# A third value tap moves from VectorE to GpSimd, and the null parts follow the subtraction for x

## What is computed

```
x = x + proj(attention(q, k, v))            # on the group-normalised x
kv = dw3x3(einsum(qkv_w, x)); k, v = split(kv)   # 3x3 depthwise convolution, nine taps per channel
q  = idwt2(dw3x3(dwt2(x)))                  # wavelets, three sets of 3x3 taps
attn = softmax(normalised q @ normalised k.T * temperature)   # 8 heads of 16 channels
```

## Time and profile before

| | us |
|---|---|
| median of 3 runs | 1373.13 |
| lowest and highest run | 1371.81, 1376.18 |
| the profiled execution, its whole time | 1372.45 |
| its span in the trace | 1370.8 |
| TensorE busy | 1157.9 |
| VectorE busy | 1008.8 |
| ScalarE busy | 803.8 |
| GpSimd busy | 533.8 |

### The profile page before, as it was taken

The page is one execution under the profiler, slowest core; times in us unless marked ns, Lnnn a source line. Parts: engine busy times, 40 slices in busy tenths (PEclk is TensorE's granted clock), DMA queues, the critical chain, the costliest instruction groups (busy, mean ns, idle before and its releaser), DMA issues. The chain is left out here.

```text
span 1370.8 us, 36304 instructions
## 1 busy us (share of the span) xinstructions
PE 1157.9 (84%) x12648; PEld 920.4 (67%) x12648; DVE 1008.8 (74%) x1801; ACT 803.8 (59%) x1414; POOL 533.8 (39%) x369
## 2 busy tenths in 40 slices
PE   0899937999999899998999999846999997999900
PEld 0555527889999899998999999724555554555500
DVE  6777517999999899998999999525777774163494
ACT  0677735777777676775777677202444445766382
POOL 6200004577687676876668686602000001000010
PEclk9999977999999999998999999866999999999955
DMA  9976783545544535445355354155777633000079
GB/s 325 416 298 262 296 196 88 138 108 123 148 106 120 136 93 147 132 99 137 98 135 144 102 132 112 40 211 185 248 262 262 231 92 121 1 0 0 1 300 406
DMA packets 148805, 221.21 MB, mean 161 GB/s; under 512 B 115746, under 2 KB 116892, under 8 KB 144296
## 3 DMA queue, kind: packets, MB, share of 16 engines
q1 hardware_dynamic: 137560, 152.23, 37.0%
q0 software_dynamic: 6480, 47.19, 9.1%
q10 hardware_dynamic: 4608, 19.67, 4.1%
HBM read 131.82 MB, written 87.20 MB: 160 GB/s over the span
## 5 line engine op out<-in xcount | busy, mean ns | idle before, releaser
L1693 PE MATMUL b_conv_bank<-b_sign,wsign 128*128 (+1 forms) x1728 | 299.7, 327 | 7.7 <-ACT b_sign L1491 7.5
L982 DVE SCALAR_TENSOR_TENSOR b_value_sum<-b_vin,b_vtaps,b_value_sum 128x576 f32<-128x576 f32 x320 | 259.3, 810 | 14.4 <-ACT b_value_sum L908 13.6
L1693 PEld LDWEIGHTS b_conv_bank<-b_sign,wsign 128*128 128x128 bf16 x1728 | 168.0, 97 | 144.6 <-issue 31.4
L936 ACT CAST b_feat<-b_bank 96x400 f16<-96x400 f32 x255 | 125.5, 492 | 184.9 <-PE b_bank L1026 184.9
L1024 PE MATMUL b_bank<-b_tkh,b_kt 96*96 96x100 f16 x1536 | 224.3, 211 | 2.5 <-DVE b_tml L1005 2.2
L1025 PE MATMUL b_bank<-b_tkl,b_kt 96*96 96x100 f16 x1536 | 223.7, 211 | 0.0
L1026 PE MATMUL b_bank<-b_tkh,b_kt 96*96 96x100 f16 x1536 | 223.7, 211 | 0.0
L1024 PE MATMUL b_bank<-b_yh,b_tmh 96*96 96x200 f16 x768 | 195.2, 254 | 30.8 <-DVE b_feat L989 11.0
L1024 PEld LDWEIGHTS b_bank<-b_tkh,b_kt 96*96 96x96 f16 x1536 | 195.2, 127 | 4.2 <-DVE b_tml L1005 2.5
L1026 PEld LDWEIGHTS b_bank<-b_tkh,b_kt 96*96 96x96 f16 x1536 | 195.3, 127 | 0.0
L1025 PEld LDWEIGHTS b_bank<-b_tkl,b_kt 96*96 96x96 f16 x1536 | 193.8, 126 | 0.0
(11 more groups left out here) (232 smaller groups left out, 2522.7 us busy)
## 6 DMA issues: line engine op xcount, KB each, us to landing
b_vin<-value_projection_scratch SPq DMA_DIRECT2D x32, 686.0 KB, 5.1
keys_scratch<-b_khl SPq DMA_DIRECT2D x24, 784.0 KB, 3.5
value_projection_scratch<-b_vout ACTq DMA_DIRECT2D x24, 784.0 KB, 4.7
b_kt<-keys_scratch SPq DMA_DIRECT2D x128, 147.0 KB, 3.3
b_xraw<-in_x SPq DMA_DIRECT2D x128, 144.0 KB, 4.8
values_scratch<-b_vacc SPq DMA_DIRECT2D x32, 576.0 KB, 3.2
values<-values_scratch SPq DMA_DIRECT2D x48, 384.0 KB, 3.7
out<-xs SPq DMA_DIRECT2D x25, 576.0 KB, 6.8
```

What stands on the lines that cost most here:

```text
L936: nc.scalar.copy(*target(n, 0, k)).then_inc(s_hi, 1)
L982: nc.vector.scalar_tensor_tensor(whole if t == DVE_TAPS[-1] else part, src, vtaps[:, t:t + 1], part, ALU.mult, ALU.add).then_inc(s_tap, 1)
L1693: ins = nc.tensor.matmul(cbank[k % NBK][:, 0:CH].rearrange("p (r c) -> p r c", c=W), p["wsign"][nth // NIMG][:, t * C:(t + 1) * C], padded ...
```

## The change

VectorE keeps taps 1 to 5 (10 instructions a group instead of 12) at an even spacing; GpSimd takes taps 6, 7 and 8 (three products and three additions a slab instead of two and two). In `body`, `low_x(i+1)` now stands ahead of `edges`.

```diff
-        DVE_TAPS = (1, 2, 3, 4, 5, 6)
-        POOL_TAPS = (7, 8)
+        DVE_TAPS = (1, 2, 3, 4, 5)
+        POOL_TAPS = (6, 7, 8)
         NTAP = 2 * len(DVE_TAPS)
         PSTEPS = 2 * len(POOL_TAPS)
-        TAP_AT = (0, 2, 3, 5, 7, 8, 10, 12, 13, 15, 17, 18)
+        TAP_AT = (0, 2, 4, 6, 8, 10, 12, 14, 16, 18)
...
                 pool.wait_ge(s_ptap, i * PSTEPS + 1)
                 pool.sem_inc(s_carry, 1)
                 add_product(slot)
-                pool.wait_ge(s_ptap, i * PSTEPS + 2)
-                pool.sem_inc(s_carry, 1)
-                product(slot, POOL_TAPS[1])
-                pool.wait_ge(s_ptap, i * PSTEPS + 3)
-                pool.sem_inc(s_carry, 1)
-                add_product(slot)
-                pool.wait_ge(s_ptap, i * PSTEPS + 4)
+                for n, t in enumerate(POOL_TAPS[1:]):
+                    pool.wait_ge(s_ptap, i * PSTEPS + (2 * n + 2))
+                    pool.sem_inc(s_carry, 1)
+                    product(slot, t)
+                    pool.wait_ge(s_ptap, i * PSTEPS + (2 * n + 3))
+                    pool.sem_inc(s_carry, 1)
+                    add_product(slot)
+                pool.wait_ge(s_ptap, i * PSTEPS + PSTEPS)
                 pool.sem_inc(s_carry, 1)
...
                     spread_taps(i + 2, k % 2)
+                if how != LAST:
+                    low_x(i + 1, (k + 1) % 2)
                 if head is not None:
                     edges(head, k // GPH % 2 ^ 1, i)
-                if how != LAST:
-                    low_x(i + 1, (k + 1) % 2)
                 first_product(i, k % 2)
```

## The result

The changed kernel takes **1412.8 us** (median of 4 runs, 1411.66 to 1421.59), against 1374.2 us for the kernel before on the same chip: a ratio of 1.0296, 95% interval 1.0251 to 1.0341. It is slower, as predicted, but by 38.6 us where the prediction had 15, and outside its range of 1379 to 1402 us.

The account below looks back on a forecast made before the run. GpSimd was taken to become the bound at 84.48 us a head: 1372.45 us profiled plus 10.2 gave 1382.7, plus 6 for the two jumps 1388.7, rounded to 1388 us; range 1379 to 1402 us.

Parts of the forecast that it names:

- GpSimd sets the pace: GpSimd's chain: the added pair costs 5.11 us, so 19.47 us a group and 84.48 us a head.
- The floor of 1382.7 us: Whole execution if GpSimd never waits after group 2: the profiled 1372.45 us plus 10.2 us.
- VectorE's relief: VectorE's two fewer instructions a group: nearly all of TensorE's 2.14 us idle time a head would go.
- The jumps: Loop's jump back before groups 12 and 20: 3 us of new GpSimd waiting at each, +6 us.
- The order at 0: Subtraction for x moved ahead of the null parts: costed at 0, bounds -2 and +2 us a head.
- taken as hidden: SyncE's load of slab i+2, ending at least 5.1 us later in its group: no cost taken.
- (d): Rival: slab load and chain bind too, 21.9 us a group with slow clocks; 1411 us with jumps, 7%.
- The slow clock in the third group at 0: TensorE's clock falling in each head's third group: taken as 0, upper bound 2 us times 7, 14 us.
- The sign for a wrong size: The prediction is wrong in size if GpSimd still waits for more than 1 us a group.

Follow-up runs that it names:

- early_load: The changed kernel with the load of slab i+2 put behind the last product of slab i's chain, ahead of the store: 1399.9 us, ratio 1.0187.
- after_unrolled_early: The changed kernel with the 24 groups of the loop written out and the slab's load behind the last product: 1385.0 us, ratio 1.0078.
- relief_only: The changed kernel with tap 6 left out altogether, so VectorE keeps 5 taps and GpSimd 2: 1366.6 us, ratio 0.9944.
- order_only: The kernel before with the subtraction for x put ahead of the null parts, taps as before: 1374.3 us, ratio 0.9999.
- half_tap: The kernel before with tap 6 split by halves between VectorE and GpSimd, and the subtraction ahead of the null parts: 1396.6 us, ratio 1.0173.
- half_early: half_tap with the next slab loaded behind the last product of a slab, ahead of its store: 1377.0 us, ratio 1.0019.
- taps_only: The changed kernel with the old order, null parts and then the subtraction for x: 1405.2 us, ratio 1.0219.
- before_early: The kernel before with the slab's load put behind the last product: 1373.3 us, ratio 0.9995.

## Why the prediction was right in direction and wrong in size

**GpSimd sets the pace: right.** 5.11 us for the pair, 19.47 us a group and 84.48 us a head were measured as 5.10 (445.82 to 450.92), 19.4 to 19.5, and 84.5 to 84.7 in the heads of early_load without a jump. The rule weighed against it (the Trainium skill, GPSIMD Engine Reference, 4.1 Engine selection), half of VectorE's speed for two inputs, would have given an estimate of 2.9 us for the pair; the measurement decides for 5.10.

**The floor of 1382.7 us: right, with some luck.** after_unrolled_early has 1385.0. That kernel has no jumps, but neither had the floor. Two errors nearly cancel in it: the subtraction for group 2 starts at 251.47 and not at 250.0, and from there to the one for group 31 it takes 607.0 us and not 610.0, since without the loop a plain group lasts 19.3 us.

**VectorE's relief: wrong in size.** It was put at nearly all of 2.14 us a head for this part alone; relief_only shows 0.73 in a head without a jump. The sum for a GpSimd that sets the pace did not use it.

**The jumps: nearly right.** 3 us of new waiting each were taken, 3.3 and 4.7 measured in early_load. In after they are 5.78 and 5.71 us; the late input falls into the same heads.

**The order at 0: right only alone.** By the medians it is 0 in order_only. In the six heads it is -5 us with the load early (515.78 against 520.68) and +8 us with it late (529.83 against 521.80). Both are within the bounds of 2 us a head, but the cause of the +8 is one that the step did not have.

**The input of the slab "taken as hidden": this is the step that failed.** It cost 14.1 us in six heads, of the 24 us that were missing in the value; without it (early_load, 1399.9 us) the time lies inside the stated range. The text had seen that the load comes at least 5.1 us later, and had a rival (d) for it, but worked that out as a mean cycle of two groups, 40.3 us against 42.2. That rival's 1411 us lies close to 1412.8 by luck: it has a slow clock in every pair of groups, and the trace has the input late once a head, with a fall of the clock behind it in two heads of six. A mean hides one group of a head. In the new order the subtraction for x, which lets TensorE go on, stands before the null parts, and the chain that releases the load still stands behind them. Counted from that subtraction, the load is later by 5.1 + 6.6 = 11.7 us. The traces show 13.9 us from the one to the other in before (394.23 to 408.17) and 25.8 in after (397.10 to 422.89). The margin could have been read from the kernel before. Its load starts at 408.17 and takes 5.1 us; ScalarE's tap 0 that reads it is this row:

```profile
418.97 0.75 ACT L908 ACTIVATE b_value_sum<-b_vin,b_vtaps 128x576 f32<-128x576 f32 x1 [0.20 <-DVE b_vacc L982]
```

10.8 us from issue to use, less 5.1, is a spare of 5.7 us. The new pair alone nearly uses it up, and with the null parts it is not enough. The same two rows in the other kernels, order_only (SyncE, ScalarE):

```profile
411.80 0.36 SPq L679 DMA_DIRECT2D b_vin<-value_projection_scratch  x1
...
418.50 0.74 ACT L908 ACTIVATE b_value_sum<-b_vin,b_vtaps 128x576 f32<-128x576 f32 x1 [0.20 <-DVE b_vacc L982]
```

half_tap:

```profile
412.91 0.35 SPq L680 DMA_DIRECT2D b_vin<-value_projection_scratch  x1
...
419.69 0.74 ACT L919 ACTIVATE b_value_sum<-b_vin,b_vtaps 128x576 f32<-128x576 f32 x1 [3.18 <-DMA b_vin<-value_projection_scratch]
```

and the kernel after:

```profile
422.89 0.35 SPq L679 DMA_DIRECT2D b_vin<-value_projection_scratch  x1
...
428.26 0.74 ACT L909 ACTIVATE b_value_sum<-b_vin,b_vtaps 128x576 f32<-128x576 f32 x1 [4.55 <-DMA b_vin<-value_projection_scratch]
```

In order_only 6.7 us are left from issue to use, and ScalarE does not wait for the input. The move delays the load by 3.6 us only (411.80 against 408.17), since a GpSimd with room makes up for the rest. In half_tap ScalarE is ready 3.6 us after the issue and waits 3.18 us; in after it is ready 0.8 us after it and waits 4.55.

**The slow clock in the third group at 0: wrong.** It was bounded by 14 us and linked to TensorE's wait for the low part of x. The six heads of after have four falls of the clock in a third group. Two come behind just that wait, at 340.81 (1.93 us) and 426.56 (1.52 us). The other two, from 522 and from 703, come behind banks held up by the late input. The six heads of after hold 13.2 us more of TensorE's busy time than those of before, early_load 4.3, so most of it came with the late input.

**The sign for a wrong size did not show.** The text named more than 1 us of waiting a group. GpSimd waits for x for 18.0 us in the six heads of after, 0.75 a group; some 5 us more lie between its steps, in waits of 1 us and less.

**What stays open.** Why half_early is 4 us above its expectation was not followed; its six heads lose 501.09 - 484.87 = 16.2 us to the loop, where the kernel before loses 11.4. Nor is it shown why the new order gains 4 to 5.5 us once the input is early. That a jump makes TensorE idle is seen, but which part of its price is the idle time and which the clock was not measured apart.

## What to carry to other kernels

When work is added to a chain, list every transfer that is released by its end, and read for each the spare time between landing and first use, in the group where it is smallest, not over a mean cycle. A reordering that costs nothing by itself may use up the same spare time as the added work; cost the two together. A load should be released by the last reader of its buffer, not by the end of the chain that this reader belongs to: that single move, which also put the load ahead of the store, was worth 13 us here and 20 us in half_tap, and next to nothing in taps_only and the kernel before, where the input was not late.

## What the runs showed of the hardware

A stop of TensorE of only 1.86 us (to 523.01) was followed by the 1.2 GHz level up to 529; the trace of before had shown 0.89 us without and 3.65 us with such a fall. The length of the stop does not settle it. In the trace of after one stop of 1.93 us was followed by the slow level and one of 1.92 us was not:

```profile
340.81 0.22 PE L1025 MATMUL b_bank<-b_ana,b_xh 96*96 96x100 f16 x1 [1.93 <-POOL b_xl L741]
...
786.31 0.22 PE L1025 MATMUL b_bank<-b_ana,b_xh 96*96 96x100 f16 x1 [1.92 <-POOL b_xl L741]
```

```profile
341.00:344.00 3.00, 3.00 (x32) 2.53 (x29) 0.00 (x0) 0.72 (x2) 2.82 (x2) 0.63 1.21 258
787.00:790.00 3.00, 3.00 (x53) 2.87 (x51) 1.50 (x3) 2.09 (x4) 2.82 (x2) 1.00 1.28 250
```

What tells the two apart is not shown by any run here.

A loop jump is dear even with three rounds: two jumps between heads cost 11.4 us in the kernel before. TensorE's idle time there is 3.65 us at the first, with no wait behind it, and 3.81 us at the second (to 628.53), which the trace puts down to VectorE. The rest lies behind them, with the clock at 0.98 of full in the mean of the six heads against 1.00 without jumps. This agrees with what the Trainium skill says (Runtime: NRT & Kernel Launch, Instruction fetch mechanics): a taken branch to a page that isn't loaded stalls on its fetch, and full unrolling is preferred where possible. No run here shows the fetch itself.

A product over half the elements took 1146 ns on GpSimd against 2107, an addition 1408 against 2638. Half a tap costs 53 to 54% of a whole one, so splitting one is cheap on this engine.

The same load of 686 KB landed 5.3 us (median) after its issue where it was issued behind the store of a slab (after), and 4.0 us after it where it was issued ahead of that store (early_load); the kernel before shows the same two figures, 5.1 and 4.0 us (before_early).
